# Spreading B by DMA instead of by matmul in a state-space and expert kernel, and dispatching sequences in groups of 1, 2, 2, 2 and 1

## The chip, the cores and the metric

One core of one Trainium2 chip. The time is the device time of one execution in microseconds. TensorE is called PE, VectorE DVE, ScalarE ACT, GpSimd POOL and SyncE SP, as in the profile.

## The reference

Eight sequences of 512 steps with 128 channels go through a selective state-space layer with 16 states and then through a layer of 8 experts, of which each token takes two. Between them stand layer norms and residual sums.

```python
def step(h, inputs):                 # one scan over the 512 steps
    a_t, bx_t, c_t = inputs
    h = a_t * h + bx_t               # a = exp(dt * A), bx = dt * B * xn
    y_t = jnp.einsum('bn,bdn->bd', c_t, h)
    return (h, y_t)
...
gate_weights = jax.nn.softmax(gate_logits, axis=-1)
topk_values, topk_indices = jax.lax.top_k(gate_weights, TOP_K)
hidden = jax.nn.relu(jnp.einsum('bsd,edh->bseh', x, w1) + b1)
expert_out = jnp.einsum('bseh,ehd->bsed', hidden, w2) + b2
...
x = x + layernorm(ssm(layernorm(x)));  x = x + layernorm(experts(layernorm(x)))
```

## The kernel before

Channels lie on the 128 partitions and time on the free axis, so one state of one sequence is one scan of 128 x 512. There are 8 x 16 = 128 of them; two make a pair `n`, and a sequence has 8 pairs. For each sequence `states` (PE) makes the rows B and C, `states_copy` (ACT) and `rest` (DVE) bring them to SBUF, `delta` (PE), `softplus` (ACT) and `dt_gx` (POOL) make `dt` and `gx = dt * xa`. Then for each state:

- `rep` (PE) spreads the row of B over the 128 partitions, by a matmul that chooses the row, into one of three PSUM banks `b_ps`. B was split for this in two parts (copy and rest), so that the matmul loses no precision.
- `drive` (DVE) multiplies the bank in place by `gx`, `decay` (ACT) makes `ab = exp(dt * A)`, `scan` (DVE) makes `hs`.
- `weigh` (POOL) multiplies the pair's `hs` by C, which was written to `c_dram` by `rows_out` (SP) and is read back by `spread`, four states at once, onto all partitions. ACT issues these reads. `reduce` (PE) adds the states in PSUM by transposes.

After a sequence come `y_stats`, `x1`, `x2` and the gate's logits. When all sequences of a group have them, the routing chain of small DVE steps (`gate_max`, `softmax`, `second`, `starts`, `slots`) gives each token its slots. POOL scatters the tokens by row DMAs (8 per sequence) to `slots_in`, which SP has cleared. The slots are cut in tiles of 128 tokens of one expert. A group of n sequences needs n x 8 + 7 tiles at most, and all are computed: `tile_load` and `tile_weights` (SP), `tile_turn` (PE), `tile_up` (PE, 8 matmul records), `tile_relu` (ACT), `tile_down` (PE, 8 records), `tile_keep` (ACT), `tile_store` (SP). When the group's tiles are stored, POOL gathers each token's two results (8 row DMAs per sequence; from the third sequence on into the memory of `c_rep`, so only after the last `weigh`), and `bias_mix` (PE), `mix` (DVE), `mix_scale`, `result` (ACT), `add` (POOL) and `store` (SP) end the sequence.

The order of the work on every engine is written out when the program is built: a planner with a cost for each step (`COST`), a time for each DMA to land (`LANDING`) and urgencies places each step on its engine, and each engine then does its list in order and waits on semaphores. Where PE would idle before the scans end, the planner puts in filling matmuls (`warm`), if a sum in `y_ps` is open or no tile has begun. Steps that share the PSUM bank `misc` are kept apart. After the last scan the banks `b_ps` also serve `tile_up`.

## Time and profile before

| | us |
|---|---|
| median of 3 runs (lowest, highest) | 542.03 (538.26, 542.36) |
| profiled execution: its time, its span | 541.83, 540.1 |
| busy: PE, DVE, ACT, POOL | 467.3, 346.1, 326.8, 306.8 |
| tiles | 92 |

The span runs from the first to the last instruction; 1.7 us of the time lie around it. Busy times are sums over the span, and the stretches below matter more than they do.

### The profile page before, as it was taken

The page shows a single profiled execution, that of the slowest core. Times are in us where ns is not written, and L with a number is a line of the kernel's source. Part 1 is how long each engine was busy: PE and PEld are TensorE (multiplying, and loading weights), DVE is VectorE, ACT ScalarE, POOL GpSimd, SP SyncE. Part 2 cuts the span into 40 slices and gives each one's busy share as a digit, 9 for nine tenths or more (in the row PEclk, how much of TensorE's full clock was granted, in tenths as well). Part 3 has the DMA queues.
Part 4 walks back from the last instruction along what each step waited for, and adds up shares of the span by engine and source line. Part 5 has one row for each costly group of instructions (what it writes and reads, how often), then busy time and mean ns, then how long its engine had stood idle before and what let it go on. Part 6 is the DMA issues. An engine that isn't in the chain of part 4 may idle for free.

```text
span 540.1 us, 9872 instructions
## 1 busy us (share of the span) xinstructions
PE 467.3 (87%) x2932; PEld 340.6 (63%) x2952; DVE 346.1 (64%) x815; ACT 326.8 (61%) x838; POOL 306.8 (57%) x229
## 2 busy tenths in 40 slices
PE   4799999998899999899999889998998999983430
PEld 1255555554445457777886767998987989971320
DVE  4389989989989989999989957623350000006551
ACT  3477575671475576787887666485676666652331
POOL 1148547372778874477976666954454454436710
PEclk9999999999999999999999989999999999995555
DMA  6694406262615476636765972387776787732211
GB/s 159 223 365 161 155 4 235 103 202 97 203 46 193 150 201 217 231 116 214 260 205 169 324 217 85 88 222 202 215 184 195 231 235 197 201 85 57 65 40 39
DMA packets 69603, 91.70 MB, mean 170 GB/s; under 512 B 6696, under 2 KB 50480, under 8 KB 65456
## 3 DMA queue, kind: packets, MB, share of 16 engines
q1 hardware_dynamic: 60848, 49.11, 32.9%
q10 hardware_dynamic: 4608, 33.56, 17.2%
q0 software_dynamic: 4096, 8.40, 4.9%
q8 instruction: 26, 0.43, 0.3%
q14 instruction: 25, 0.20, 0.1%
HBM read 72.43 MB, written 18.61 MB: 169 GB/s over the span
## 4 chain that ended last, share of the span: by engine, by line
PE 69%; DVE 11%; issue 9%; ACT 7%; SPq 1%; DMA 1%; DVEq 0%; another core or an unknown queue 0%; POOLq 0%; POOL 0%; ACTq 0%
PE out_ps L1184 13%; PE y_ps L1090 9%; PE b_ps L1074 9%; PE y_ps L1148 9%; PE hid_ps L1172 8%; PE out_ps L1148 6%; PE b_ps L1172 5%; ACT hid_t L778 4%; PE misc L1142 2%; DVE hs L858 2%; PE misc L1065 1%; PE misc L1061 1%; PE misc L1106 1%; ACT mix L796 1%; DVE st L817 1%
## 5 line engine op out<-in xcount | busy, mean ns | idle before, releaser
L590 POOL TENSOR_TENSOR ch<-hs,c_rep 128x1024 f32<-128x1024 f32 x64 | 151.0, 2362 | 78.8 <-DVE hs L858 74.9
L858 DVE TENSOR_TENSOR_SCAN hs<-ab,b_ps 128x512 f32<-128x512 f32 x128 | 151.9, 1205 | 0.2
L730 ACT ACTIVATE ab<-dt,decay 128x512 f32<-128x512 f32 x128 | 90.3, 720 | 57.4 <-DVE hs L858 55.3
L1184 PE MATMUL out_ps<-w_f,hid_t 128*128 x736 | 101.4, 281 | 9.9 <-ACT ot L786 4.9
L849 DVE TENSOR_TENSOR b_ps<-b_ps,gx 128x512 f32<-128x512 f32 x128 | 86.5, 685 | 25.5 <-PE b_ps L1074 18.7
L1184 PEld LDWEIGHTS out_ps<-w_f,hid_t 128*128 128x128 f32 x736 | 89.6, 191 | 18.9 <-issue 17.1
L606 POOL DMA_INDIRECT slots_in<-x,pos x64 | 63.2, 987 | 38.8 <-PE out_ps L1184 11.8
L778 ACT ACTIVATE hid_t<-hid_ps,w_tile 128x128 f32<-128x128 f32 x224 | 63.7, 371 | 30.7 <-PE hid_ps L1172 19.9
L618 POOL DMA_INDIRECT c_rep<-slots_out,pos x48 | 45.4, 945 | 44.7 <-PE out_ps L1184 31.7
L1148 PE MATMUL y_ps<-none 128*128 128x512 bf16 x242 | 66.9, 382 | 1.5 <-issue 1.0
L983 DVE SCALAR_TENSOR_TENSOR mix<-c_rep,weight,misc 128x128 f32<-128x128 f32 x24 | 6.7, 343 | 95.5 <-PE misc L1134 90.8
L1074 PE MATMUL b_ps<-b_rows,choose 64*128 64x512 f32 x128 | 61.5, 493 | 6.8 <-DVE b_rows L839 3.5
L1090 PE MATMUL y_ps<-ident,ch 128*128 128x128 f32 x512 | 67.4, 275 | 0.0
L1090 PEld LDWEIGHTS y_ps<-ident,ch 128*128 128x128 f32 x512 | 59.4, 142 | 7.4 <-issue 1.6
L1172 PE MATMUL hid_ps<-xt_t,w_tile 128*128 128x128 f32 x448 | 61.2, 280 | 2.2 <-ACT hid_t L778 1.1
L1172 PEld LDWEIGHTS hid_ps<-xt_t,w_tile 128*128 128x128 f32 x448 | 54.4, 191 | 7.5 <-issue 7.5
L778 ACT ACTIVATE hid_t<-b_ps,w_tile 128x128 f32<-128x128 f32 x144 | 41.0, 372 | 25.0 <-PE b_ps L1172 11.6
L1074 PEld LDWEIGHTS b_ps<-b_rows,choose 64*128 64x128 f32 x128 | 23.1, 185 | 40.1 <-issue 19.4
L1172 PE MATMUL b_ps<-xt_t,w_tile 128*128 128x128 f32 x288 | 38.8, 279 | 1.7 <-issue 0.7
L1148 PEld LDWEIGHTS y_ps<-none 128*128 128x128 bf16 x259 | 21.1, 98 | 30.0 <-issue 17.1
L1148 PE MATMUL out_ps<-none 128*128 128x512 bf16 x142 | 37.7, 406 | 1.4 <-DVE zeros L1007 1.3
L1172 PEld LDWEIGHTS b_ps<-xt_t,w_tile 128*128 128x128 f32 x288 | 34.8, 191 | 3.8 <-issue 3.5
(131 smaller groups left out, 481.6 us busy)
## 6 DMA issues: line engine op xcount, KB each, us to landing
c_rep<-c_dram ACTq DMA_DIRECT2D x32, 1024.0 KB, 4.7
w_tile<-w_rows SPq DMA_DIRECT2D x92, 258.0 KB
slots_in<-zeros SPq DMA_DIRECT2D x4, 1472.0 KB, 8.6
slots_out<-ot SPq DMA_DIRECT2D x44, 128.0 KB
xt<-slots_in SPq DMA_DIRECT2D x20, 256.0 KB
x<-x SPq DMA_DIRECT2D x8, 256.0 KB, 4.5
out<-mix SPq DMA_DIRECT2D x8, 256.0 KB
slots_in<-x,pos POOLq DMA_INDIRECT x64
```

What stands on the lines that cost most here:

```text
L590: nc.gpsimd.tensor_tensor(ch[:, n % NCH], hs[:, n % NH], c_rep[:, r // 2, 2 * (r % 2):2 * (r % 2) + 2].rearrange("p n t -> p (n t)"), ALU. ...
L606: nc.gpsimd.indirect_dma_start(out=slots_in[g], out_offset=bass.IndirectOffsetOnAxis(pos[:, r // K, K * b + r % K:K * b + r % K + 1], 0), ...
L618: nc.gpsimd.indirect_dma_start(out=yg(b)[:, r, :], out_offset=None, in_=slots_out[g], in_offset=bass.IndirectOffsetOnAxis(pos[:, r // K, K ...
L730: nc.scalar.activation(ab[:, i % NA], dt[:, b % 2], ACT.Exp, scale=decay[:, 2 * r + h:2 * r + h + 1]).then_inc(s["decayed"], 1)
L778: last = nc.scalar.activation(hid_t[:, q % NHT, c * P:(c + 1) * P], hidden(q)[:, c * P:(c + 1) * P], ACT.Relu, bias=w_tile[:, q % NW, HID ...
L849: nc.vector.tensor_tensor(b_ps[i % NBX][:], b_ps[i % NBX][:], gx[:, b % 2], ALU.mult).then_inc(s["driven"], 1)
L858: nc.vector.tensor_tensor_scan(hs[:, n % NH, h * T:(h + 1) * T], ab[:, i % NA], b_ps[i % NBX][:], 0.0, ALU.mult, ALU.add).then_inc(s["scan ...
L1074: nc.tensor.matmul(b_ps[i % NBX][:], choose[:, 2 * r + h:2 * r + h + 1].to_broadcast([64, P]), b_rows[:, b % 2], start=True, stop=True).th ...
L1090: last = nc.tensor.matmul(y_ps[:, k * P:(k + 1) * P], ch[:, n % NCH, h * T + k * P:h * T + (k + 1) * P], ident[:], start=False, stop=(r == ...
L1148: nc.tensor.matmul(y_ps[:] if y_open else out_ps[:], none[:], none[:, 0:1].to_broadcast([P, T]), start=not y_open, stop=not y_open)
L1172: last = nc.tensor.matmul(hidden(q)[:, c * P:(c + 1) * P], w_tile[:, q % NW, c * P:(c + 1) * P], xt_t[:, m % NB, j * P:(j + 1) * P], start ...
L1184: last = nc.tensor.matmul(out_ps[:, j * D:(j + 1) * D], hid_t[:, q % NHT, c * P:(c + 1) * P], w2_f[:, bass.ds(e * HC * D + c * D, D)], sta ...
```

## The change

B is spread by DMA, as C was. `states` now makes 32 rows in one form, one copy (`rows_copy`, ACT) takes them to SBUF, `rows_out` writes B and C to DRAM, and `b_spread` (SP) reads two rows for each pair onto all partitions (512 KB) into one of four buffers `b_rep`. `rep`, `rest`, the choosing matrix and the splitting are gone. `spread` moves from ACT's queue to SP's. `gx` is made by DVE in a PSUM bank of its own, `gx_ps`, one for all sequences, and POOL keeps only the sum `dt_add`. `drive` reads B from SBUF and `gx_ps` and writes one of two banks `u_ps`; it waits for the scan two before. The groups are 1, 2, 2, 2 and 1 sequences, which makes 15 + 3 x 23 + 15 = 99 tiles. The second weights are loaded after the second sequence's scans, not at the first scan, and each group's clear some pairs later. The planner's costs are changed in many places.

```diff
-GROUPS = (2, 2, 2, 2)
+GROUPS = (1, 2, 2, 2, 1)
-NBX = 3
+NU = 2
+NBR = 4
+NLATE = NU + 1
...
-HOP = 0.12
+HOP = 0.18
...
-    "PE": "turn turn_u states delta rep reduce gate_turn gate_logits count weigh_turn bias_mix tile_turn tile_pick tile_up tile_down",
-    "POOL": "dt_gx weigh scatter gather add",
-    "SP": "weights_2 clear rows_out tile_weights tile_load tile_store store",
+    "PE": "turn turn_u states delta reduce gate_turn gate_logits count weigh_turn bias_mix tile_turn tile_pick tile_up tile_down",
+    "POOL": "dt_add weigh scatter gather add",
+    "SP": "weights_2 clear rows_out b_spread spread tile_weights tile_load tile_store store",
...
-    at(0, "weights_2", 0, 0, scan_of(0))
+    at(0, "weights_2", 0, 0, scan_of(2 * PAIRS))
     for g in range(len(GROUPS)):
-        at(5, "clear", g, 0, scan_of(PAIRS * FIRST[g] + 1))
+        at(5, "clear", g, 0, scan_of(PAIRS * FIRST[g] + 6))
...
-        at(2, "rest", b, 0, ("states_copy", b, 0))
-        at(2, "delta", b, 0, ("rest", b, 0), ("dt_gx", b - 1, 0))
+        at(2, "delta", b, 0, ("rows", b, 0))
+        at(1, "gx", b, 0, ("dt_add", b, 0), ("drive", n0 - 1, 1))
...
+            at(1, "b_spread", n, 0, ("rows_out", b, 0), ("drive", n - NBR, 1))
             for h in range(2):
-                at(1, "rep", n, h, ("rest", b, 0), ("scan", *before(n, h, NBX)))
-                at(3, "drive", n, h, ("rep", n, h), ("dt_gx", b, 0))
+                at(3, "drive", n, h, ("b_spread", n, 0), ("gx", b, 0), ("scan", *before(n, h, NU)))
...
+            def b_spread(n, _):
+                b, r = n // PAIRS, n % PAIRS
+                if r == 0:
+                    sp.wait_ge(rows_stored[b % 2], 16 * (b // 2 + 1))
+                after(sp, s["driven"], 2 * (n - NBR + 1))
+                sp.dma_start(b_rep[:, n % NBR].rearrange("p n t -> p (n t)"),
+                             rows_dram[b % 2][2 * r:2 * r + 2, :].rearrange("n t -> (n t)")[None, :]
+                             .to_broadcast([P, 2 * T])).then_inc(b_loaded[n % NBR], 16)
+
+            def spread(b, q):
+                if q == 0:
+                    sp.wait_ge(rows_stored[b % 2], 16 * (b // 2 + 1))
+                after(sp, s["weighed"], PAIRS * (b - 1) + 2 * (q + 1))
+                sp.dma_start(c_rep[:, q].rearrange("p n t -> p (n t)"),
...
-            def rest(b, _):
-                dve.wait_ge(s["b_hi_ready"], b + 1)
-                nc.vector.tensor_tensor(b_rows[32:64, b % 2], misc[32:64, :], b_rows[32:64, b % 2].bitcast(F32),
-                                        ALU.subtract).then_inc(s["b_ready"], 1)
+            def gx(b, _):
+                dve.wait_ge(s["dt_ready"], b + 1)
+                after(dve, s["driven"], N * b)
+                nc.vector.tensor_tensor(gx_ps[:], dt[:, b % 2], xa[:, b % 2], ALU.mult).then_inc(s["gx_ready"], 1)
...
+                if h == 0:
+                    dve.wait_ge(b_loaded[n % NBR], 16 * (n // NBR + 1))
                 if r == 0 and h == 0:
                     dve.wait_ge(s["gx_ready"], b + 1)
-                dve.wait_ge(s["b_rep"], i + 1)
-                nc.vector.tensor_tensor(b_ps[i % NBX][:], b_ps[i % NBX][:], gx[:, b % 2], ALU.mult).then_inc(s["driven"], 1)
+                after(dve, s["scanned"], i - NU + 1)
+                nc.vector.tensor_tensor(u_ps[i % NU][:], b_rep[:, n % NBR, h], gx_ps[:], ALU.mult).then_inc(s["driven"], 1)
...
-                nc.tensor.matmul(b_ps[i % NBX][:], choose[:, 2 * r + h:2 * r + h + 1].to_broadcast([64, P]),
-                                 b_rows[:, b % 2], start=True, stop=True).then_inc(s["b_rep"], 1)
```

## Rows read from the trace of the kernel before

**Rows 1.** The page: busy shares, and the span in 40 equal slices, in tenths.
```profile
PE 467.3 (87%) x2932; PEld 340.6 (63%) x2952; DVE 346.1 (64%) x815; ACT 326.8 (61%) x838; POOL 306.8 (57%) x229
...
PE   4799999998899999899999889998998999983430
...
DVE  4389989989989989999989957623350000006551
...
DMA  6694406262615476636765972387776787732211
```

**Rows 2.** Stretches: start:end, length, busy (instructions) by engine, granted clock, DMA share, GB/s.
```profile
27.00:345.40 318.40, 304.32 (x1754) 199.56 (x1772) 287.11 (x532) 209.16 (x459) 210.28 (x123) 0.99 0.54 179
345.40:485.50 140.10, 131.17 (x1077) 123.48 (x1076) 20.60 (x97) 91.55 (x313) 69.73 (x71) 1.00 0.71 192
485.50:540.10 54.60, 15.88 (x68) 11.50 (x68) 26.68 (x108) 15.31 (x42) 22.75 (x22) 0.53 0.18 50
```

**Rows 3.** Stretches for line 1172, the up matmuls of the tiles: PE, PEld.
```profile
0.00:344.00 344.00, 33.87 (x248) 30.08 (x248) 1.00 0.55 180
...
344.00:486.00 142.00, 65.92 (x488) 58.98 (x488) 1.00 0.70 191
```

**Rows 4.** Timeline: start, duration; the first and last scatter of group 0, the first tile.
```profile
136.44 1.17 POOL L606 DMA_INDIRECT slots_in<-x,pos  x1 [4.57 <-DVE expert L974]
...
187.42 0.96 POOL L606 DMA_INDIRECT slots_in<-x,pos  x1 [0.30 <-issue]
...
208.26 1.06 PE L1172 MATMUL hid_ps<-xt_t,w_tile 128*128 128x128 f32 x8
```

**Rows 5.** Timeline of the start, several engines.
```profile
16.43 0.34 SPq L525 DMA_DIRECT2D c_dram<-c_rows  x1
...
17.96 0.68 DVE L839 TENSOR_TENSOR b_rows<-misc,b_rows 32x512 fp32r<-32x512 f32 x1
...
18.02 2.12 ACTq L708 DMA_DIRECT2D c_rep<-c_dram  x4
...
20.28 2.07 PE L1065 MATMUL misc<-xa,w_dt 128*128 128x512 f32 x2
...
27.64 1.90 DVE L849 TENSOR_TENSOR b_ps<-b_ps,gx 128x512 f32<-128x512 f32 x3 [6.23 <-POOL gx L581]
```

**Rows 6.** DMA: queues, issues with KB and us to landing, and two stretches.
```profile
q10 hardware_dynamic: 4608, 33.56, 17.2%
...
c_rep<-c_dram ACTq DMA_DIRECT2D x32, 1024.0 KB, 4.7
...
slots_in<-zeros SPq DMA_DIRECT2D x4, 1472.0 KB, 8.6
...
56.00:58.00 2.00, 2.00 (x10) 0.80 (x9) 1.41 (x2) 0.72 (x1) 1.44 (x1) 1.00 0.98 397
420.00:440.00 20.00, 18.79 (x153) 17.40 (x152) 0.00 (x0) 12.84 (x45) 9.73 (x11) 1.00 0.89 248
```

**Rows 7.** Waits from 28 to 344 us: total, times, longest.
```profile
DVE b_ps L849 <- PE b_ps L1074: 18.7, 31, 3.5
```

**Rows 8.** Groups by line (busy, mean ns), and line 849 alone (min/median/max ns).
```profile
L858 DVE TENSOR_TENSOR_SCAN hs<-ab,b_ps 128x512 f32<-128x512 f32 x128 | 151.9, 1205 | 0.2
...
L1074 PE MATMUL b_ps<-b_rows,choose 64*128 64x512 f32 x128 | 61.5, 493 | 6.8 <-DVE b_rows L839 3.5 <-DVE hs L858 3.0
...
L839 DVE TENSOR_TENSOR b_rows<-misc,b_rows 32x512 fp32r<-32x512 f32 x8 | 5.5, 683 | 1.2 <-ACT b_rows L699 1.0
...
L849 DVE TENSOR_TENSOR b_ps<-b_ps,gx x128: 661/685/700, 27.6 to 342.5; 128x512 f32<-128x512 f32 x128
```

**Rows 9.** Timeline and stretches (DVE, then its scans alone) of group 0's routing; all four.
```profile
120.84 2.34 POOL L590 TENSOR_TENSOR ch<-hs,c_rep 128x1024 f32<-128x1024 f32 x1 [1.89 <-DVE hs L858]
...
121.14 2.12 DVE L917 TENSOR_TENSOR prob<-r_exp,r_sum 128x64 f32<-128x64 f32 x1
...
118.00:137.00 19.00, 18.01 (x45) 1.00 0.29 111
...
118.00:137.00 19.00, 3.86 (x4) 1.00 0.29 111
...
L974 DVE TENSOR_SCALAR expert<-exp_f x4: 164/165/166, 136.0 to 385.3; 1x23 int32<-1x23 f32 x4
```

**Rows 10.** Timeline of the tail.
```profile
486.63 1.12 DVE L983 SCALAR_TENSOR_TENSOR mix<-c_rep,weight,misc 128x128 f32<-128x128 f32 x4 [83.68 <-PE misc L1134]
...
503.21 2.85 DVE L989 SCALAR_TENSOR_TENSOR mix<-c_rep,weight,mix 128x128 f32<-128x128 f32 x4
...
510.23 0.94 POOL L618 DMA_INDIRECT c_rep<-slots_out,pos  x1 [0.30 <-issue]
...
524.99 1.12 DVE L983 SCALAR_TENSOR_TENSOR mix<-c_rep,weight,misc 128x128 f32<-128x128 f32 x4 [2.36 <-PE misc L1134]
```

More of the change, by code:

```diff
@@ L80 @@
 COST = {
-    "stats": 1.8, "shift_all": 0.3, "rest": 0.7, "drive": 0.66, "scan": 1.22, "y_stats": 1.8, "x1": 3.6, "x1_shift": 0.25,
-    "gate_bias": 0.25, "gate_max": 0.6, "softmax": 2.1, "second": 2.0, "starts": 2.4, "slots": 2.2, "mix": 5.2,
-    "mix_shift": 0.5,
-    "scales_all": 0.9, "norm": 1.6, "norm_u": 1.6, "skip_copy": 0.65, "channels": 0.75, "states_copy": 1.25, "spread": 0.1, "softplus": 2.8,
-    "decay": 0.72, "y_scale": 0.55, "x1_scale": 0.55, "x2": 1.6, "gate_copy": 0.65, "gate_exp": 0.3, "weigh_copy": 0.65,
@@ L86 @@
-    "mix_scale": 0.55, "result": 1.7, "tile_copy": 0.65, "tile_relu": 1.15, "tile_keep": 0.42,
-    "turn": 0.5, "turn_u": 0.5, "states": 1.0, "delta": 1.0, "rep": 0.38, "reduce": 1.0, "gate_turn": 0.5, "gate_logits": 1.1,
-    "count": 0.8, "weigh_turn": 0.5, "bias_mix": 1.2, "tile_turn": 0.5, "tile_pick": 0.05, "tile_up": 1.0, "tile_down": 1.0,
-    "dt_gx": 3.3, "weigh": 2.45, "scatter": 1.25, "gather": 1.25, "add": 1.3,
-    "weights_2": 0.4, "clear": 0.4, "rows_out": 0.4, "tile_weights": 0.6, "tile_load": 0.4, "tile_store": 0.4,
+    "stats": 1.3, "shift_all": 0.3, "gx": 1.0, "drive": 0.62, "scan": 1.16, "y_stats": 1.3, "x1": 2.7, "x1_shift": 0.2,
@@ new lines @@
+    "gate_bias": 0.25, "gate_max": 0.6, "softmax": 2.3, "second": 2.1, "starts": 2.6, "slots": 1.7, "mix": 3.7,
+    "mix_shift": 0.4,
+    "scales_all": 0.9, "norm": 1.6, "norm_u": 1.6, "skip_copy": 0.6, "channels": 0.7, "rows": 0.62, "spread": 0.4, "softplus": 2.7,
+    "decay": 0.63, "y_scale": 0.6, "x1_scale": 0.6, "x2": 1.6, "gate_copy": 0.5, "gate_exp": 0.3, "weigh_copy": 0.5,
+    "mix_scale": 0.6, "result": 1.4, "tile_copy": 0.5, "tile_relu": 1.1, "tile_keep": 0.35,
+    "turn": 0.46, "turn_u": 0.46, "states": 0.9, "delta": 0.9, "reduce": 0.9, "gate_turn": 0.46, "gate_logits": 0.9,
@@ L432, in program @@
         nb_f = sb("nb_f", [P, K])
-        b_ps = [bank(f"b_ps{i}") for i in range(NBX)]
+        u_ps = [bank(f"u_ps{i}") for i in range(NU)]
+        gx_ps = bank("gx_ps")
         y_ps = bank("y_ps")
```

122 lines of the change are left out of this document (51 added, 71 removed).

## The prediction

> **What bounds the kernel now.** I read the page first, for the shares of the engines [rows 1]: TensorE (PE) is busy almost all the time until slice 36, VectorE (DVE) until slice 26, and neither share says which of them sets the end. So I cut the span into stretches [rows 2]. From 27 to 345.4 us DVE is busy 287.1 of 318.4 us: this is the stretch of the 128 scans, and DVE bounds it. From 345.4 to 485.5 us PE is busy 131.2 of 140.1 us and DVE hardly works: expert tiles that were left over. From 485.5 to 540.1 us no engine is busy half the time: a chain of small steps at a granted clock near 0.5 (1.2 GHz).
>
> The count of tile matmuls divides the backlog [rows 3]: a tile has 8 up matmuls, so 248 before 344 us are 31 tiles, and 488 after it are 61 of the 92. One leftover tile costs 141/61 = 2.31 us. The first tile starts only at 208.3 us [rows 4], so in the scan stretch a tile comes every (344 - 208.3)/31 = 4.4 us. From these numbers the time is: end of the scans, plus 2.31 us for each tile not yet done, plus the tail.
>
> **The start.** Before, PE computes the gate input's matmul `delta` only at 20.28 us, because it waits for `rest` on DVE, which stands behind seven `stats` steps until 17.96 us [rows 5]. After, `delta` waits for the copy of `rows` alone, which ends near 15.8 us, so `delta` can run at 16.0: 4.3 us earlier, and the steps behind it (softplus on ScalarE (ACT), the sum on GpSimd (POOL)) move with it. `gx` goes from POOL (1.26 us) to DVE (0.69 us, as `drive`). The first drive starts at 27.6 now. I count -4.3 and leave the 0.6 of `gx` as cover for the new path that must be done by then: `rows_out` takes 18.02 - 16.43 = 1.6 us until the queue behind it goes on, and the first load of B then has until 23.3. A megabyte lands in 4.7 us [rows 6], half of one should in less: 15.8 + 1.6 + 0.4 + 4.7 = 22.5, late by nothing. If it were queued behind all of C (another 4 MB), the gain would be gone: bounds 0 and -5.
>
> **The scan stretch on DVE**, by terms:
> - `rep` goes. DVE waited 18.7 us in 31 pieces for it [rows 7]: -18.7. What is late next is the load of B, below.
> - `rest` goes (7 of its 8 lie here, 0.683 us: -4.8) and `gx` comes (7 of 8, taken at the 0.685 us of a `drive`: +4.8) [rows 8]. Zero together.
> - `gx` reads both inputs from SBUF. Of the small DVE steps with two SBUF inputs one took 2.12 us where the median sibling takes 0.23, and it ended exactly with the `weigh` on POOL that had begun at 120.84 [rows 9]. A `gx` can be held the same way. POOL is busy 66% of the stretch [rows 2], and half of a 2.36 us `weigh` is 1.2: 7 x 0.66 x 1.2 = +6; bounds 0 and 7 x 1.9 = 13. `drive` itself keeps one input in PSUM in both kernels; its 128 durations lie within 661 to 700 ns [rows 8], so it isn't held and costs the same.
> - A fourth routing chain falls in this stretch (groups 0 to 3 now end before the last sequence; three did before). One takes DVE 18.0 us between 118 and 137, less the scans (3.9) and four drives (2.8) in it: 11.3 us [rows 9]. The added one is that of a group of one sequence: half as wide, and most of its steps are fixed cost, so +9; bounds 7 and 13.
> - The load of B must not be late. A buffer is refilled when the second drive of pair n-4 is done and is needed at pair n: three pairs of 2 x (1.21 + 0.69) us and a scan, 12.6 us. Against this stand 4.7 us or less of landing, plus whatever is ahead of it in the same queue: a clear takes 8.6, a C load 4.7 [rows 6]. One in front fits or nearly fits, two don't. I take +5 for the five clears, the load of the second weights and a few waits of SP's in-order list; bounds 0 and 40.
>
> Who else is behind SP's new waits: SP now holds `b_spread` and `spread` in one list with tile weights, tile loads and stores. If an earlier entry waits for ACT or PE, the B load behind it waits too, with the 12.6 us as its cover; a C load that waits for POOL's `weigh` now holds B and the tile weights, where it used to hold ACT. ACT loses the 0.33 us issue of each C load and one of two copies, neither on the path. Sum of the stretch with the start: -4.3 - 18.7 + 6 + 9 + 5 = -3: the scans end at 342.4 instead of 345.4.
>
> **The backlog.** The tiles become 15 + 3 x 23 + 15 = 99, seven more than 4 x 23. So it has to be seen how many are done by 342.4. A sequence takes 40 us, beginning at 23.3. Routing was finished at 136.1 (two sequences end near 107) and, for the last group, at 385.5, 40 us behind its last scan [rows 9]; I take 37. The 16 scatters of a group took 51 us beside `weigh` (136.4 to 187.4), and the first tile came 21 us later [rows 4]. For the new groups this gives: group 0 (after one sequence) routed near 100, its 8 scatters done near 126, its 15 tiles done before 210. Group 1 (after three) routed at 180, scattered at 231, first tile at 245. Group 2 (after five) routed at 260, scattered at 311, ready near 326. Group 3 is ready only after the scans.
> The pace within a supply: 4.4 us a tile now; `rep` frees 16 x 0.49 = 7.8 us of PE in a sequence [rows 8], and a tile costs PE 2.2 us, so at best 3.2 us a tile; I take 3.7, since ACT has 3 us more to do as well. Group 1's 23 tiles then last until 330, and 3 or 4 of group 2 follow: 15 + 23 + 4 = 42 done, 57 left against 61. That is -4 x 2.31 = **-9**. The bounds: at 4.4 us a tile 37 are done, 62 left, +2; with the first tile at once behind the scatters and 3.2 us each 47 are done, 52 left, -21. The hidden half of this: PE has nothing but filling matmuls between 210 and 245, and what is freed there buys nothing. The cover: 19 tiles of group 2 last 44 us beyond the scans, and group 3's scatters need some 35; if they come later, PE idles.
>
> **The tail.** Six `mix` steps follow each other from 486.6 to 525.0, 7.7 us apart, because each needs the one PSUM bank `misc` [rows 10]; the last result is at 531.3 and POOL's drain takes 8.6. The last group has 8 gathers now instead of 16 in this stretch. They don't release the mixes (the last gather is at 510.2, its mix at 525.0), but two of the six second halves took 2.7 and 2.9 us instead of 1.1 beside them [rows 10]. One such goes: -1.7; the planner's order of the rest I can't see; bounds -9 (one mix moves under the tiles) and +8 (one more in the tail). I take -2.
>
> **The sum** against the profiled execution, 541.8 us with a span of 540.1: -3 - 9 - 2 = -14, **528 us**. The median of the runs is 542.0, the same.
>
> **A rule on loads.** All DMA packets took 0.54 of the engines' time from 27 to 345.4 [rows 2]. C took 17.2% of 540 us = 93 us for 33.6 MB [rows 6]; B is as large: another 93. With eleven more tiles (0.71 x 140/61 = 1.6 us each) and seven more tiles of clears it is 172 + 93 + 18 + 3 = 286 of 319 us, 0.90. A C load alone filled 0.98 at 397 GB/s, while tile traffic filled 0.89 at 248 GB/s [rows 6]. So the room is small. The Trainium skill ("DMA: Bandwidth & Descriptors", "Measured (HBM→SBUF, 128 partitions, SWDGE, issued from GpSimd)") asks for DMAs of at least 1 MiB for 75% of the peak; a B load is half of that. If B cost 1.3 times what C costs for its bytes, which is an estimate from that page's table, the need would be 0.98 and the second rival below would decide; this trace has only loads of a full megabyte from such a source.
>
> The hold of a two-input step by POOL is also what the Trainium skill says ("GPSIMD Engine Reference", its table of specifications: the SBUF interfaces are shared with VectorE, with contention for instructions with two SBUF inputs). By that rule `gx` is held and `drive` isn't, which is how the term of +6 was made from rows.
>
> **Rivals.**
> 1. *More gain (0.18).* Tiles start right behind their scatters, PE runs at 3.2 us a tile, and DVE's new waits are nil. For it: the first tile came 21 us after its scatters by order, not by need. Scans end at 337, 47 done: -8 - 21 - 2 = -31, **511 us**.
> 2. *Slower: DMA becomes the bound (0.22).* B and C together need 186 us of the 16 engines in a stretch of 319, on one in-order queue with clears and tile weights; DVE then waits for B in the place where it waited for `rep`. It decides when the engines sustain less than 286/319 = 0.90 of their time usefully. At 0.80 the stretch lasts 286/0.80 = 357, 38 us more: the scans end near 381, with perhaps four tiles more done: 541.8 + 35 - 9 - 9 - 2 = **557 us**. For it: the page's DMA line already has 9 tenths in slice 22 and 7 in slices 19 and 23 [rows 1]. Against it: C lands in 4.7 us beside all this.
> 3. *Nothing comes of it (0.15).* DVE's waits move elsewhere (decay on ACT, B), the seven more tiles eat the earlier start: **542 us**.
>
> **Chances.** The forecast 0.45, the rivals as given. The forecast's own range is 516 to 540; the whole range reaches to rival 1 and to rival 2: 504 to 557. A measurement of this kernel tells about 1% from nothing. Faster by over 1% (under 536.6): most of the forecast and rival 1, 0.6. Within 1%: rival 3 and the edge, 0.17. Slower: 0.23.
>
> **What would show it.** DVE's waits for PE before `drive` gone and little put in their place by the DMA of B; first drive near 23; last scan near 342; tile matmuls (8 each) before the last scan near 42 x 8; first tile near 145 and a gap without tiles between 210 and 245; DMA share near 0.9 in the scans; six mixes behind the last tile. A wait of DVE for the B load of more than 15 us in all, or a last scan beyond 350, speaks for rival 2. The forecast is wrong at its weakest place if the tile supply differs: ten tiles are 23 us.

## The result, and the profile after

The kernel after takes 544.9 us (median of 11 runs, 542.9 to 547.4) against 539.1 for the kernel before (11 runs, 537.8 to 542.4): a ratio of 1.010, 95% interval 1.008 to 1.013. The change makes the kernel slower by 1%. The profiled execution of after took 546.6 us, its span 543.9.

First the three stretches of [rows 2], cut again at the end of the last scan and of the last tile: start:end, length, busy (instructions) on PE, PEld, DVE, ACT and POOL, granted clock, DMA share, GB/s. Then the same view for the up matmuls alone, as in [rows 3].

```profile
23.30:362.00 338.70, 289.01 (x1852) 214.05 (x1852) 284.78 (x551) 213.74 (x503) 204.56 (x119) 0.90 0.82 282
362.00:498.00 136.00, 125.80 (x1038) 118.85 (x1038) 27.76 (x132) 90.19 (x306) 68.33 (x68) 1.00 0.72 196
498.00:543.90 45.90, 12.87 (x56) 9.39 (x56) 21.64 (x90) 12.78 (x35) 21.55 (x21) 0.55 0.19 55
```

```profile
0.00:362.00 362.00, 48.66 (x337) 44.96 (x337) 0.89 0.80 275
362.00:498.00 136.00, 61.05 (x456) 54.84 (x456) 1.00 0.72 196
```

337/8 = 42 tiles are done when the scans end and 456/8 = 57 are left, the forecast's numbers. One costs 136/57 = 2.39 us (2.31 forecast), and the tail is 45.9 us (52.6 forecast: the span before less 485.5, less 2). What misses is the first row: the scans last 338.7 us and not 319.1. DVE is busy 284.8 us of them, less than forecast; it idles 53.9. Against the span that the forecast implied, 528 - 1.7 = 526.3, the three give +19.6 + 57 x 0.08 - 6.7 = +17.5; the span is 17.6 longer.

The waits of DVE in that stretch (total us, times, longest), to hold against [rows 7]:

```profile
DVE st_y L822 <- PE y_ps L1086: 22.9, 5, 12.8
DVE logit L894 <- PE misc L1102: 9.7, 5, 4.5
...
DVE u_ps L856 <- DMA b_rep<-rows_dram: 5.1, 4, 3.7
DVE gx_ps L845 <- POOL dt L603: 4.4, 1, 4.4
DVE nb L887 <- ACT rs L669: 4.1, 2, 3.5
```

The 18.7 us for `rep` are gone as forecast, and the load of B takes 5.1 of them back, also as forecast. But `st_y`, which reads what PE sums up from POOL's `weigh`, now waits 22.9 us in five pieces. Two places show what is behind it. The same stretch view for two windows of 40 us:

```profile
103.00:143.00 40.00, 30.57 (x212) 23.57 (x211) 29.72 (x47) 24.94 (x58) 22.47 (x12) 0.87 0.99 339
183.00:223.00 40.00, 25.65 (x121) 15.95 (x120) 24.50 (x48) 18.53 (x38) 23.38 (x16) 0.74 0.85 287
```

DVE loses 10.3 us in the first and 15.5 in the second. Here is the first in the timeline (start, duration, engine, line, idle time before it and what ended it; SPq is SP's DMA queue):

```profile
104.29 0.88 SPq L515 DMA_DIRECT2D w_f<-w  x1
...
105.21 11.17 SPq L538 DMA_DIRECT2D b_rep<-rows_dram  x1
...
117.46 1.05 SPq L568 DMA_DIRECT2D xt<-slots_in  x2
...
121.42 1.29 DVE L856 TENSOR_TENSOR u_ps<-b_rep,gx_ps 128x512 f32<-128x512 f32 x2 [3.74 <-DMA b_rep<-rows_dram]
...
124.28 1.12 PE L1138 MATMUL misc<-ident,xt 128*128 128x128 f32 x4 [9.16 <-DMA xt<-slots_in]
```

The 2 MB of the second weights (`w_f`, 15.8 us to landing) are issued just ahead of the first tiles of the small first group, and the entry of SP behind them, a load of B, is held 11.2 us at its issue. B is 3.7 us late, and PE stands 9.2 us at the first tile, whose load is further back in the same list: the matmuls for `y_ps` are behind it in PE's list. The second place is a ring through five lists:

```profile
175.07 0.67 DVE L856 TENSOR_TENSOR u_ps<-b_rep,gx_ps 128x512 f32<-128x512 f32 x1
...
175.79 0.45 SPq L520 DMA_DIRECT2D slots_in<-zeros  x1
...
176.29 13.12 SPq L538 DMA_DIRECT2D b_rep<-rows_dram  x1
...
177.35 0.27 ACT L791 ACTIVATE ot<-out_ps 128x128 f32<-128x128 f32 x1
...
189.45 0.45 SPq L575 DMA_DIRECT2D slots_out<-ot  x1
...
194.68 1.01 POOL L640 DMA_INDIRECT yg_first<-slots_out,pos  x1 [16.96 <-issue]
...
197.00 2.35 POOL L612 TENSOR_TENSOR ch<-hs,c_rep 128x1024 f32<-128x1024 f32 x1
...
199.40 1.97 PE L1086 MATMUL y_ps<-ident,ch 128*128 128x128 f32 x8 [12.72 <-POOL ch L612]
...
201.40 0.69 DVE L822 BATCH_NORM_STATS2 st_y<-y_ps 128x6 f32<-128x128 f32 x3 [12.85 <-PE y_ps L1086]
```

The last tile of group 0 is copied by ACT at 177.6, ready to be stored. Its store stands in SP's list behind a load of B (pair 35), and the issue of that load holds SP for 13.1 us. So the store goes out at 189.45; POOL, which has come to the first gather of sequence 0, has idled 17.0 us for it; the `weigh` behind the gather runs at 197.0, PE's `y_ps` at 199.4, and DVE goes on at 201.4. From the store on nothing in this chain is slow: each engine waits for the next entry of another one's list.

What holds the load of B isn't its buffer. The `drive` that frees it is the one at 175.07, over before the load's issue begins (a wait for a buffer stands in this profile as idle time ahead of an entry, not in its duration: 100.1 us in 31 pieces for the loads of B). What stands right ahead of it is the clear of group 2 (175.79, 1.4 MB, 16.7 us to landing), and until SP gets past the load the DMA engines are full:

```profile
176.30:189.40 13.10, 9.84 (x56) 5.40 (x55) 11.84 (x26) 9.00 (x19) 1.41 (x2) 1.00 1.04 383
```

The first place is of the same kind: the buffer of the load at 105.21 was free at 102.1, and the second weights stand ahead of it. In the scans of after, the entries right behind the four clears and behind the second weights are held 7.3, 9.4, 11.2, 13.1 and 7.4 us at a DMA share of 1.00 to 1.05; of SP's other 283 issues after 19 us only one took over 1.5 us (3.0).

### The profile page after: what moved, and what is told of

Its sections match the earlier page's. It is cut to its first block, busy times and chain, and to the rows that moved or that the text cites. A ratio compares the mean times of both kernels' runs of the same rounds, so it can differ in the third digit from the quotient of the medians.

```text
span 543.9 us, 10219 instructions
## 1 busy us (share of the span) xinstructions
PE 438.1 (81%) x2967; PEld 345.7 (64%) x2967; DVE 346.7 (64%) x852; ACT 327.9 (60%) x865; POOL 297.4 (55%) x218
## 4 chain that ended last, share of the span: by engine, by line
PE 43%; DVE 17%; issue 16%; DMA 9%; ACT 7%; SPq 3%; POOL 2%; POOLq 0%; DVEq 0%; ACTq 0%
PE out_ps L1180 10%; PE hid_ps L1168 7%; PE y_ps L1086 6%; PE y_ps L1144 5%; DVE u_ps L856 5%; DMA w_tile<-w_rows 5%; DVE hs L865 4%; PE u_ps L1168 3%; ACT hid_t L783 2%; PE gx_ps L1168 2%; POOL ch L612 2%; PE misc L1138 2%; DMA c_rep<-rows_dram 2%; PE misc L1067 2%; DVE run L951 1%
## 5 line engine op out<-in xcount | busy, mean ns | idle before, releaser
L865 DVE TENSOR_TENSOR_SCAN hs<-ab,u_ps 128x512 f32<-128x512 f32 x128 | 150.3, 1205 | 0.6 <-DVE u_ps L856 0.5
L735 ACT ACTIVATE ab<-dt,decay 128x512 f32<-128x512 f32 x128 | 88.8, 722 | 34.2 <-DVE hs L865 33.6
L1144 PE MATMUL y_ps<-none 128*128 128x512 bf16 x378 | 93.9, 386 | 0.0
L856 DVE TENSOR_TENSOR u_ps<-b_rep,gx_ps 128x512 f32<-128x512 f32 x128 | 83.3, 681 | 5.5 <-DMA b_rep<-rows_dram 5.1
L1086 PEld LDWEIGHTS y_ps<-ident,ch 128*128 128x128 f32 x512 | 62.4, 149 | 26.7 <-POOL ch L612 23.3
L1144 PEld LDWEIGHTS y_ps<-none 128*128 128x128 bf16 x378 | 37.9, 101 | 37.2 <-issue 4.2
L990 DVE SCALAR_TENSOR_TENSOR mix<-c_rep,weight,misc 128x128 f32<-128x128 f32 x24 | 6.7, 343 | 57.3 <-issue 41.6
L783 ACT ACTIVATE hid_t<-u_ps,w_tile 128x128 f32<-128x128 f32 x92 | 26.3, 372 | 14.1 <-issue 7.6
L640 POOL DMA_INDIRECT yg_first<-slots_out,pos x16 | 15.6, 974 | 26.9 <-issue 22.1
L791 ACT ACTIVATE ot<-out_ps 128x256 f32<-128x256 f32 (+1 forms) x52 | 19.8, 380 | 16.0 <-PE out_ps L1180 14.5
L1138 PE MATMUL misc<-ident,xt 128*128 128x128 f32 x99 | 16.5, 291 | 15.4 <-DMA xt<-slots_in 9.2
L776 ACT ACTIVATE xt_t<-misc 128x512 f32<-128x512 f32 (+1 forms) x26 | 15.4, 593 | 17.4 <-PE misc L1138 17.1
L1168 PE MATMUL u_ps<-xt_t,w_tile 128*128 128x128 f32 x184 | 24.7, 278 | 0.9 <-ACT hid_t L783 0.6
## 6 DMA issues: line engine op xcount, KB each, us to landing
slots_in<-zeros SPq DMA_DIRECT2D x3, 1472.0 KB, 16.7
```

What stands on the lines that cost most here:

```text
L640: nc.gpsimd.indirect_dma_start(out=yg(b)[:, r, :], out_offset=None, in_=slots_out[g], in_offset=bass.IndirectOffsetOnAxis(pos[:, r // K, K ...
L735: nc.scalar.activation(ab[:, i % NA], dt[:, b % 2], ACT.Exp, scale=decay[:, 2 * r + h:2 * r + h + 1]).then_inc(s["decayed"], 1)
L783: last = nc.scalar.activation(hid_t[:, q % NHT, c * P:(c + 1) * P], hidden(q)[:, c * P:(c + 1) * P], ACT.Relu, bias=w_tile[:, q % NW, HID ...
L856: nc.vector.tensor_tensor(u_ps[i % NU][:], b_rep[:, n % NBR, h], gx_ps[:], ALU.mult).then_inc(s["driven"], 1)
L865: nc.vector.tensor_tensor_scan(hs[:, n % NH, h * T:(h + 1) * T], ab[:, i % NA], u_ps[i % NU][:], 0.0, ALU.mult, ALU.add).then_inc(s["scann ...
L1086: last = nc.tensor.matmul(y_ps[:, k * P:(k + 1) * P], ch[:, n % NCH, h * T + k * P:h * T + (k + 1) * P], ident[:], start=False, stop=(r == ...
```

## The experiments

Eighteen kernels ran. The ratio is to the kernel before on the same chip, with its 95% interval. Scans is when the last scan ends, idle is what DVE isn't busy between the first scan and that time, left is the tiles not yet done then (from the up matmuls), and the last column is the span; these four are of one profiled execution each. ([rows 3] counts 61 left for before, at 344 us; one more tile is done by 345.4.)

| kernel | ratio | scans | idle | left | span |
|---|---|---|---|---|---|
| before | 1 | 345.4 | 30.7 | 60 | 540.1 |
| after | 1.010 [1.008, 1.013] | 362.0 | 53.9 | 57 | 543.9 |
| e_b_dma_only | 0.947 [0.944, 0.950] | 329.2 | 22.0 | 56 | 511.2 |
| e_groups_only | 1.009 [1.006, 1.012] | 354.6 | 31.4 | 60 | 545.1 |
| e_gather_late | 0.988 [0.985, 0.992] | 347.8 | 32.7 | 55 | 529.6 |
| e_c_on_act | 0.977 [0.974, 0.980] | 344.7 | 33.3 | 56 | 526.7 |
| e_store_on_act | 0.997 [0.995, 1.000] | 353.8 | 43.3 | 57 | 537.5 |
| e_half_b | 0.993 [0.990, 0.996] | 351.7 | 42.9 | 57 | 534.9 |
| e_old_costs | 1.031 [1.029, 1.033] | 373.0 | 56.9 | 53 | 557.3 |
| e_all_three | 0.961 [0.959, 0.963] | 338.5 | 27.0 | 53 | 518.8 |
| e_late_act | 0.996 [0.995, 0.998] | 362.0 | 50.2 | 51 | 542.6 |
| e_b_only_late | 0.954 [0.952, 0.957] | 329.4 | 20.7 | 55 | 514.7 |
| e_w2_early | 0.999 [0.996, 1.001] | 356.9 | 45.4 | 57 | 538.7 |
| e_no_filler | 1.000 [0.997, 1.002] | 357.3 | 47.3 | 57 | 539.0 |
| e_hop_17 | 1.015 [1.012, 1.019] | 362.8 | 42.8 | 55 | 539.8 |
| e_hop_20 | 1.003 [1.000, 1.006] | 353.2 | 41.6 | 55 | 530.7 |
| e_b_hop_20 | 0.949 [0.945, 0.952] | 327.1 | 20.8 | 56 | 505.9 |
| e_before_hop_14 | 1.031 [1.028, 1.034] | 361.0 | 38.8 | 61 | 548.5 |
| e_split_last | 0.971 [0.968, 0.974] | 335.5 | 23.7 | 60 | 525.6 |
| e_hop_20_w2 | 0.976 [0.971, 0.981] | 346.4 | 34.8 | 55 | 528.6 |

The four kernels with `hop` in their name but without `w2` ran on a chip on which the kernel before took 531.4 us (13 runs); on the others it took 539.1 to 541.6 in the median. Across chips the ratios are compared, and with some caution.

**The two halves of the change.** e_b_dma_only is the kernel after, e_groups_only the kernel before, each with one line changed:

```
e_b_dma_only   -GROUPS = (1, 2, 2, 2, 1)
               +GROUPS = (2, 2, 2, 2)
e_groups_only  -GROUPS = (2, 2, 2, 2)
               +GROUPS = (1, 2, 2, 2, 1)
```

> The changed kernel with the groups of before, 2, 2, 2 and 2 (92 tiles); the planner lays out a new order for it. Theory 1 (a ring of waits through the early gather): group 0 is stored only after its 23 tiles and no gather of sequence 0 lies ahead of POOL's weigh in the scans, so the 12.9 us stall near 190 us is gone; seven tiles fewer are 16 us in any case; time near 515 to 525. Theory 2 (DMA is the bound in the scans): the DMA share of the scans stays above 0.8, DVE idles some 50 us there as in the changed kernel, and only the seven tiles are won: 528 to 535. Theory 3 (it is the groups alone that cost): 520 or less, faster than the kernel before.

> The kernel before with the groups 1, 2, 2, 2 and 1 and nothing else. If the groups are what costs, this is slower than before by about 5 to 12 us (seven tiles are 16 us, more of them done in the scans gives some back): 545 to 552. If the loads of B are what costs, this is at 540 or less.

B by DMA alone gains 5.3%: 28 us of 541. The groups alone lose 0.9%. By the product of the ratios the change should give 0.956, and it gives 1.010: the halves cost some 29 us more together than apart. The scan stretch of B alone, and its longest waits of DVE:

```profile
23.40:329.20 305.80, 277.30 (x1790) 200.87 (x1816) 283.79 (x533) 207.04 (x474) 202.04 (x115) 0.96 0.88 305
```

```profile
DVE st_y L822 <- PE y_ps L1086: 6.5, 2, 4.7
DVE st_y L822 <- issue: 4.4, 1, 4.4
...
DVE u_ps L856 <- DMA b_rep<-rows_dram: 0.7, 1, 0.7
```

All the B and C there is goes through SP's queue here too, at a DMA share of 0.88 and 305 GB/s, higher than in the kernel after (0.82, 282), and DVE waits 0.7 us for B. So the loads of B as such aren't what is slow. Nor does being held behind a clear or the second weights cost much by itself: the load of B behind them is held here too, five times, 34 us in all (10.0 at the longest), but no tile load that PE stands at and no store that POOL waits for is behind it. Theory 3 for this kernel holds (512.7, under 520); of theory 2 only the high DMA share came, without its idle time. The groups alone came as expected (546.5).

**Links of the ring, one at a time.** Each of the four is the kernel after with one edit. e_gather_late plans no gather before the last `weigh`; e_c_on_act issues the C loads from ACT's list; e_store_on_act keeps all lists in order, but ACT issues each tile's store right behind the copy; e_half_b loads one row of B in place of two, and the drive of the second state reads the first one's row, so that part of the computation is changed.

```
e_gather_late   -("gather", b, r, *([("weigh", END - 1, 0)] if b >= NYG else []),
                +("gather", b, r, ("weigh", END - 1, 0),
e_c_on_act      -"spread": 0.4      "SP": "... b_spread spread tile_weights ..."
                +"spread": 0.1      "ACT": "... rows spread softplus ..."
e_store_on_act  +act.wait_ge(s["tile_copied"], m + 1)      (in tile_keep, with the store's
                +nc.scalar.dma_start(slots_out[g]..., ot...)   DMA; SP's tile_store goes)
e_half_b        -rows_dram[b % 2][2 * r:2 * r + 2, :]      b_rep[:, n % NBR, h]
                +rows_dram[b % 2][2 * r:2 * r + 1, :]      b_rep[:, n % NBR, 0]
```

> The changed kernel; the planner may place no gather before the last weigh (before, the first two sequences were free of this). Theory 1: POOL's 17 us wait for a tile store and DVE's 12.9 us wait behind it go: scans end near 349 instead of 362, time 532 to 537. Theory 2 (DMA bound) and theory 3 (PE's half clock in the scans): scans end at 358 or later, 542 to 546.

> The changed kernel with the loads of C issued from ACT's list, as before the change, so that SP's list holds no wait for weigh. If SP's in-order waits cost, some 5 to 10 us go: 534 to 540. If the bytes are what costs, the same 128 MB flow and the time stays within 3 us of 545.

> The changed kernel with every list in the order of the changed kernel, but each tile store is issued by ACT right behind the copy that it stores, not by SP. Theory 1 (SP's list holds a tile store behind a load of B that waits for DVE, POOL's early gather waits for the store, weigh waits behind the gather, and DVE for the sum of weigh): the 12.9 us wait near 190 us goes with the gather at its early place: scans end near 349, time 530 to 536. If it is the gather's own place on POOL that costs, little changes: 541 to 546.

> The changed kernel with half the bytes of B: each load brings one row (256 KB) and both drives of the pair read it, so the second state's drive uses the wrong row of B. Order and waits are as in the changed kernel. If DMA engines full of B are what the scans wait for, the 5 us of waits for B, the 9 us for the tile load and part of the sums' lateness go: scans end 15 us or more earlier, time near 528. If the order of the waits is the cause, the stall near 190 us stays and the time is 538 to 545.

Taking the early gathers out ends the scans 14.2 us earlier, moving the C loads 17.3, sending the stores by another queue 8.2. In the last, which keeps all lists, the store is issued at 179.8, but POOL still idles 9.1 us at the first gather and not 17.0: the gather runs at 188.4, beside the same clear. That is less than its theory asked for (353.8 and 539.4, not 349 and 530 to 536). Half of B's bytes, also with all lists kept, gives back 10.3 us, yet the hole at 183 stays: DVE is busy 26.0 of 40 us from 183 to 223, POOL idles 15.9 us at the gather, and the load of B behind the clear is held 12.6 us where it was 13.1. So the second hole isn't made by B's bytes. In e_gather_late that load is held 13.7 us, and DVE is still busy 36.3 us of the same stretch: the hold costs this much only where POOL has come to the gather. The first two edits also gave the planner another problem, and all lists came out in another order. With the C loads on ACT the first gather came only at 225.6 us, so that the ring was open in that kernel whatever the C loads did. What of these gains is the edit and what is the order can't be read from them alone, as e_late_act showed later.

**The planner's costs, and all three edits together.** e_old_costs plans the kernel after with the durations of before for the steps that both have, and HOP 0.12; e_all_three has B by DMA with groups of two, the late gathers, and the C loads on ACT.

```
e_old_costs  -"stats": 1.3, ... "drive": 0.62, "scan": 1.16, ... HOP = 0.18
             +"stats": 1.8, ... "drive": 0.66, "scan": 1.22, ... HOP = 0.12
```

> The changed kernel planned with the costs of the kernel before for every step that both have. The planned order is then laid out for slower engines: in its list the first gather of sequence 0 comes later. If the new costs make the plan too tight for what the engines do, this is faster than the changed kernel, 535 to 543; if they are an improvement that the groups hide, slower, 550 or more.

> B by DMA with the groups 2, 2, 2 and 2, no gather planned before the last weigh, and the loads of C issued by ACT. If what the two repairs took from the changed kernel was stalls that the groups of before also have, about 5 us go from the version with B by DMA alone: 504 to 509. If they repaired only what the groups did, it stays at 510 to 515.

The old costs make it 2% slower than after: the new ones weren't the fault. The three edits on top of each other give 0.961, a smaller gain than B by DMA alone (0.947), and 520.2 us, which is outside both of the times expected. The edits that helped the kernel after do nothing for B alone, and its scans end 9 us later.

**The rest of the idle time.** e_late_act joins the edits of e_gather_late and e_c_on_act. e_b_only_late has groups of two and late gathers. e_w2_early and e_no_filler are the kernel after with:

```
e_w2_early   -at(0, "weights_2", 0, 0, scan_of(2 * PAIRS))
             +at(0, "weights_2", 0, 0, scan_of(0))
e_no_filler  +if not walking:       (once the start is over, no filling matmuls)
              nc.tensor.matmul(y_ps[:] if y_open else out_ps[:], none[:], ...)
```

> The kernel after, with no gather planned before the last weigh and with the C loads issued from ACT's list. Alone, the first ended the scans 14.2 us earlier than in the kernel after (347.8 against 362.0), the second 17.3 us earlier (344.7). Theory (one ring of waits: a pair can only go on when ACT, SP, POOL and DVE have each come to its entry, and each edit takes one link out of the same ring): the two don't add; the scans end near 342 and the time is 522 to 528. Rival (two separate stalls): they add; the scans end near 331, five more tiles are left over, and the time is 512 to 518.

> B by DMA with the groups of before (2, 2, 2, 2), and no gather planned before the last weigh. With these groups the version without the edit ran at 512.7 and ended its scans at 329.2. Theory (it is the groups of 1, 2, 2, 2, 1 that put a whole sequence of gathers among the first scans, behind a chain that is short of time): here there is little to win; within 4 us of 512.7. Rival (a gather on POOL ahead of a weigh costs the scans in any order of groups): the scans end 10 us earlier or more, and the time is under 508.

> The kernel after, with the 2 MB load of the second weights at the first scan, as before the change, and not at the third sequence, where its issue at 104.3 us was followed by a 9.2 us wait of PE for the first tile load of group 0 (until 124.3), an 8.5 us wait of POOL behind it and a 3.7 us wait of DVE for B. Theory: those waits come from the 2 MB in front of the small loads, so the scans end 4 to 9 us earlier and the time is 536 to 541. Rival (the chain of the first group is itself late there, and the load only covers it): within 2 us of 545. Second rival: the load now lies in front of the first C and B loads, and costs the start what it gives back at 120: 543 to 550.

> The kernel after, without the filling matmuls that PE runs where its list has nothing to do, once the start is over. They serve no output; they only keep PE busy. It prices the granted clock in the scans (0.90 on average, 0.63 to 0.8 in several slices). Theory A (PE at half its clock is part of the ring: y_ps late for DVE): the clock falls to 0.7 or lower in the scans, the scans end 10 us later or more, and the time is 555 or above. Theory B (the low clock is only the trace of PE waiting for the others): the clock falls as much and the scans still end within 4 us of 362, the time within 5 us of 545.

e_late_act refuted both of its theories: two edits that alone ended the scans at 347.8 and 344.7 end them together at 362.0, where they were without either. That put in doubt every experiment in which the lists had been written anew. e_b_only_late did as expected (0.954, 3.6 us off).

e_w2_early is free of that doubt: PE's, DVE's, ACT's and POOL's lists are the same as in after, and in SP's only this load has moved. Its three windows that matter:

```profile
23.00:63.00 40.00, 32.05 (x159) 18.41 (x162) 34.17 (x49) 24.41 (x48) 22.30 (x10) 0.83 0.97 355
103.00:143.00 40.00, 36.20 (x260) 28.37 (x262) 37.58 (x74) 33.81 (x83) 26.57 (x14) 1.00 1.04 372
183.00:223.00 40.00, 25.98 (x135) 15.94 (x137) 27.00 (x48) 17.49 (x33) 29.02 (x18) 0.79 0.82 254
```

The hole from 103 to 143 is gone (37.6 us busy in place of 29.7). 3.6 us of it are paid at the start (34.2 in place of 37.8), where DVE now waits for B 4.9 us at 45.5, and the ring at 183 is untouched (27.0): 5.1 us net, as expected (the time, 541.4, is just outside the 536 to 541). The hold moved with the weights: the load of B behind them, at 27.1 us, is now the one that is held, for 13.3 us. For the second weights this shows the cause; no run moved a clear.

e_no_filler answers for the granted clock. Its scan stretch:

```profile
23.90:357.30 333.40, 222.04 (x1438) 185.45 (x1439) 286.07 (x551) 213.44 (x502) 206.26 (x119) 0.78 0.84 287
```

Without the filling matmuls the clock falls from 0.90 to 0.78 in the scans, not as far as either theory had it, and they end 4.7 us earlier, not later. DVE is busy 29.5 and 26.2 us in the two windows of the holes (29.7 and 24.5 with them). So the low clock at the holes is their trace, not their cause.

**Only the order.** In four kernels nothing but the planner's HOP differs, and with it the order in all five lists.

```
e_hop_17, e_hop_20   after:         HOP = 0.18  ->  0.17, 0.20
e_b_hop_20           e_b_dma_only:  HOP = 0.18  ->  0.20
e_before_hop_14      before:        HOP = 0.12  ->  0.14
```

> The kernel after, its lists of work written out anew with one number of the planner changed: the time that it adds between engines (HOP) is 0.17 and not 0.18. No work, no engine and no dependence changes; only the order in the lists does. Until now each edit that was meant to take away one wait also reordered the lists, and two that gained 10 and 17 us gained 5 together. Theory (the order that the planner happens to write decides some 10 us, and with it the sign of the change): the time differs from 544.9 by 5 us or more. Rival (the order is of no account; the extra idle time comes from the fourth routing chain and from the loads): within 3 us of 544.9.

> The kernel after with HOP 0.20 in the planner, nothing else. Theory (order decides): off from 544.9 by 5 us or more, in either direction, and not the same as the version with 0.17. Rival: within 3 us of 544.9.

> B by DMA with the groups of before (2, 2, 2, 2), HOP 0.20. The version with 0.18 ran at 512.7. Theory A (the gain of B by DMA is in the hardware's work, not in one lucky order): within 6 us of 512.7. Theory B (that version had a lucky order): 520 or above.

> The kernel before with HOP 0.14 and not 0.12, nothing else. Theory (any plan of this kernel has some 10 us of scatter by order): off from 541.5 by 3 us or more. Rival (the long wait for PSUM at every step set the pace of before, and the order was of little account): within 2 us of 541.5.

On one and the same chip the orders 0.17 and 0.20 of after differ by 8 us (540.7 and 532.8), with scans that end 9.6 us apart. By ratio they stand 0.5% and 0.7% on either side of after, 3 and 4 us: less than the 5 us that the theory asked for. The kernel before is more sensitive than expected: another order costs it 3.1%. B alone isn't (0.947 and 0.949). So an order is worth 1 to 3%, and the 1% by which after is slower than before lies within that, as does the 0.9% of the groups alone. The cost of the new groups *with* B by DMA doesn't: three orders with them give 1.003, 1.010 and 1.015, two with groups of two 0.947 and 0.949. No kernel with a small first group came below 0.976, in any order or with any edit; none with B by DMA and groups of two came above 0.961.

In both orders the window from 103 to 143 looks much as in after (DVE busy 31.8 us with 0.17 and 29.4 with 0.20, DMA share 1.00 and 0.99), while the ring at 183 is gone (35.3 and 36.6 us busy): the first gather comes at 245.0 and 241.8 us, not at 194.7. The two windows of e_hop_20:

```profile
103.00:143.00 40.00, 30.84 (x201) 24.19 (x202) 29.38 (x47) 23.91 (x55) 22.32 (x12) 0.87 0.99 340
...
183.00:223.00 40.00, 35.53 (x194) 21.20 (x195) 36.59 (x61) 22.91 (x44) 33.46 (x21) 0.91 0.96 326
```

So the first hole comes with the small first group in all three orders, as long as the second weights are loaded there, and the second is an accident of one.

**Which of the groups.** e_split_last has four routing chains in the scans and a last group of one sequence, as after, but a first group of two. e_hop_20_w2 is e_hop_20 with the second weights loaded at the second sequence; the other instructions keep their order.

```
e_split_last  -GROUPS = (1, 2, 2, 2, 1)
              +GROUPS = (2, 2, 2, 1, 1)
e_hop_20_w2   -at(0, "weights_2", 0, 0, scan_of(2 * PAIRS))
              +at(0, "weights_2", 0, 0, scan_of(PAIRS + 0))
```

> The kernel after with groups of 2, 2, 2, 1 and 1 sequences: four routing chains lie inside the scans, as with 1, 2, 2, 2, 1, and the last group has one sequence, but the first tiles come only behind the second sequence, as in B alone (first tile near 184). Theory (it is the early tile traffic of a first group of one sequence, beside the first B and C loads and the second weights, that costs the scans): no stretch of 40 us in which DVE is busy under 34 before 183 us; scans end near 340, ratio to before 0.965 to 0.985. Rival (each further chain of routing costs the scans some 15 us, wherever it lies): scans end at 350 or later, ratio 1.0 or above.

> The kernel after with HOP 0.20, and the 2 MB load of the second weights issued at the second sequence's first scan (near 62 us) and not at the third's (near 103 us); all the other instructions keep the order of the version with HOP 0.20, which has the same hole there (DVE waits 4.5 us for B at 121.7, busy 29.4 of 40 us from 103 to 143, DMA share 0.99), and a DMA share of 0.69 from 63 to 103. Theory: the 8 us come back and nothing is lost at the start: scans end near 346, ratio to before 0.985 to 0.992. Rival (the loads ahead of the B loads only shift the wait to 63 to 103): ratio within 0.003 of that version's 1.003.

The scan stretch of e_split_last, and its longest wait of DVE:

```profile
23.40:335.50 312.10, 284.53 (x1832) 207.94 (x1858) 288.44 (x551) 210.23 (x486) 204.72 (x117) 0.97 0.87 302
```

```profile
DVE st_y L822 <- PE y_ps L1086: 11.5, 3, 5.6
```

The theory's ratio (0.965 to 0.985) holds with 0.971, and in no window of 40 us before 183 is DVE busy less than 38 us. The scans end at 335.5, which is 6.3 us later than in B alone: 4.7 us of work (288.4 busy against 283.8) and 1.7 of idle time. That is what the fourth routing costs the scans in this one order; its last step comes at 346.8, behind them. The other 18 to 27 us (353.2, 362.0 and 362.8 against 335.5) come with the small *first* group. e_hop_20_w2 fills the first hole (DVE busy 37.6 of 40 us from 103 to 143, 29.4 before the edit) and ends the scans 6.8 us earlier, at 346.4 as expected; its ratio is better than expected (0.976), but the two ran on different chips, and their spans differ by 2.1 us only. Even so 11 us to e_split_last remain. The longest of DVE's waits is then another one, that of the routing for PE's gate logits:

```profile
DVE logit L894 <- PE misc L1102: 16.2, 4, 4.7
```

In e_split_last that wait is 3.3 us. A small first group has its first tile at 129 us and not at 184, so PE's list holds tile matmuls in the stretch of the next group's routing, where it otherwise holds filling matmuls. That this is what makes the logits late is argued from the lists; no run here took it away alone.

## Why the prediction was wrong

**B by DMA.** This half was right, and its terms are borne out. The first drive runs at 22.1 us (forecast 23.3). The wait for `rep` went and nothing of its size came: DVE waits 0.7 us for B in B alone, 5.1 in after (forecast 5). The scans of B alone end at 329.2; by the forecast's terms without the added chain it would be 342.4 - 9 = 333.4. The hold of `gx` by POOL was sized too high: +6 forecast, 8 x (0.933 - 0.685) = 2 us in after (3.8 in B alone, where the mean is 1.154 us). The mechanism is there, and `drive`, with one input in PSUM, isn't held (667 to 697 ns). The trace agrees on both with the sharing rule of the Trainium skill ("GPSIMD Engine Reference", its table of specifications). The group of `gx` and the durations (min/median/max) of `drive`:

```profile
L845 DVE TENSOR_TENSOR gx_ps<-dt,xa 128x512 f32<-128x512 f32 x8 | 7.5, 933 | 7.8 <-POOL dt L603 7.8
```

```profile
L856 DVE TENSOR_TENSOR u_ps<-b_rep,gx_ps x128: 667/682/697, 22.1 to 359.7; 128x512 f32<-128x512 f32 x128
```

**The added routing chain.** Forecast +9 with bounds 7 and 13; e_split_last shows 6.3, just under the lower bound. The forecast put the whole of it into the scans. The trace has the last step of a routing, `expert`, for the fourth group only at 371.4, behind the last scan (first and last start stand in the row: 85.8 is group 0, 400.1 group 4):

```profile
L981 DVE TENSOR_SCALAR expert<-exp_f x5: 160/165/167, 85.8 to 400.1; 1x23 int32<-1x23 f32 x3, 1x15 int32<-1x15 f32 x2
...
371.36 0.17 DVE L981 TENSOR_SCALAR expert<-exp_f 1x23 int32<-1x23 f32 x1
```

DVE's work in the scans is 17 us below what the forecast implied (319.1 less 17 of idle time makes 302; 284.8 are measured). The two terms account for 4 and at most 9 of it. The 17 us are a gain, which the idle time ate more than twice over.

**The step that failed** is the last term of the scan stretch, "+5 for the five clears, the load of the second weights and a few waits of SP's in-order list; bounds 0 and 40". DVE idles 30.7 us in the scans of before, of which 18.7 are `rep`: 12.0 were other. The forecast thus allowed 12 + 5 = 17 for after; there are 53.9. The term measured 42, just past its upper bound. It failed for two reasons.

First, it looked for the price at the B load alone: "a clear takes 8.6", against a cover of 12.6 us, and "one in front fits or nearly fits". For B that was nearly right, 5.1 us show up there. But a clear or the second weights hold SP itself, 7 to 13 us at the next entry, and with it all that stands behind: tile loads, for which PE waits, and tile stores, for which POOL's gathers wait; and the scans wait for PE's `y_ps` and POOL's `weigh`. The trace of before has the sign of it, at the start, where the clear stands right behind the second weights and its issue takes 6.9 us:

```profile
16.98 0.87 SPq L514 DMA_DIRECT2D w_f<-w  x1
17.89 6.91 SPq L519 DMA_DIRECT2D slots_in<-zeros  x1
```

Second, it was sized without the other half of the change: with groups of two the same term measures 22.0 - 12.0 = 10 us, and there the first tiles come at 184 us and not at 129. The prediction had named the mechanism ("if an earlier entry waits for ACT or PE, the B load behind it waits too") with the roles reversed: in the worst place it is the B load that is held, behind a clear, and the tile's store that is behind it.

**The backlog.** 42 done and 57 left, exactly as forecast, but by luck. Group 0 was routed at 85.8 us (forecast 100) and its first tile came at 128.7 (145). Its 15 tiles had their up matmuls by 173, and the next came at 268.7 (245), a gap of 96 us where 35 were foreseen. PE and PEld for the up matmuls alone:

```profile
180.00:268.00 88.00, 0.00 (x0) 0.00 (x0) 0.82 0.75 257
```

Group 1 started 24 us later than forecast, and the scans ended 20 us later, so nearly the same number fitted in. The early start of the tiles pays for the seven added ones and no more: B alone, without it, leaves 56 tiles, after leaves 57, and the groups alone leave 60, as many as before. What wasn't counted is that it puts tile traffic beside the scans at a time when DVE otherwise is busy 38.6 of 40 us, as in B alone:

```profile
103.00:143.00 40.00, 35.50 (x193) 19.53 (x197) 38.60 (x88) 18.65 (x36) 23.98 (x16) 1.00 0.77 261
```

**The tail.** -2 forecast, -8.7 measured: five mixes are behind the last tile and not six, which the bound of -9 stood for ("one mix moves under the tiles").

**The rivals.** Rival 2 gave the sign, and its mechanism in places only. Over the scans DMA isn't the bound: the share is 0.82, below B alone's 0.88, and 0.82 x 338.7 = 278 us of transfers compare with the 286 forecast. But in the first four stretches in which SP is held, 41 us together, it is 1.00 to 1.05. The page's rule on DMAs of at least 1 MiB (the Trainium skill, "DMA: Bandwidth & Descriptors", "Measured (HBM→SBUF, 128 partitions, SWDGE, issued from GpSimd)") didn't show: loads of 512 KB beside C reach 374 GB/s from 23 to 63 us, and half the bytes of B left the ring where it was. Its tests were half right: the last scan beyond 350 came, the 15 us of waiting for B didn't. Rival 3 (542) was nearest in the number, and DVE's waits did move elsewhere, though not to where it said: to `y_ps` and the logits, and hardly to `decay` or B.

What stays open: 11 to 30 us more idle time of DVE with a small first group than in e_split_last, of which the move of the second weights recovers 5 to 7 and a luckier order about 9; whether the remainder is the tile matmuls ahead of the gate logits; and what clears placed elsewhere, or on another queue, would give back, which no run tried. That the result is *slower* by 1% and not equal is a matter of the one order that was planned, on either side; what is shown of the change is that its first half is worth 5% and that the small first group takes it back.

## What to carry to other kernels

Judge each half of a change in a kernel of in-order lists by itself, and the pair again: B by DMA alone, with groups of two, is the best version here (0.947), and the groups cost 6.7% with it (1.010/0.947) and 0.9% without it. When a load that waits for a buffer moves into a list, follow not only the load but each entry behind it to the engine that waits for that entry; the price turns up elsewhere, as a wait for another engine. Look in the queue's own rows at how long each issue takes, and at what stands right ahead of a long one: here the clears and the second weights, which nobody waits for, held the list. And before an edit of a planned kernel is credited with one or two per cent, replan the unedited one with a neutral number changed.

## What the runs showed that was not expected

- A neutral reordering of the lists moved the kernel before by 3.1%; two orders of after stand 1.5% apart on one chip; the ratio of B alone moved by 0.2%.
- The filling matmuls don't pay in the scans: without them the granted clock there is 0.78 and not 0.90, and the ratio to before is 1.000 where after has 1.010.
- One chip ran the kernel before in 531.4 us (530.7 to 533.7, 13 runs), 1.8% faster than the others did.
- With B's loads beside them, C landed in 6.7 us (4.7 in [rows 6]) and a clear in 16.7 (8.6). Sharing SP's queue needn't be the cause for C: issued by ACT it landed in 7.3 and 7.4 us (e_all_three, e_late_act).

```profile
c_rep<-rows_dram SPq DMA_DIRECT2D x32, 1024.0 KB, 6.7
...
slots_in<-zeros SPq DMA_DIRECT2D x3, 1472.0 KB, 16.7
```
